# An attention kernel's steps in a new order: written out for all sixteen heads in place of one repeated turn

## The chip, the cores and the metric

One core of one Trainium2 chip. The time is that of the whole program on the device, in microseconds (us), the median of the runs; less is better. The five engines of the core each run a list of instructions in its order: TensorE (PE, with its weight loads as PEld), VectorE (DVE), ScalarE (ACT), GpSimd (POOL) and SyncE (SP), which here only starts transfers. They wait for one another by semaphores.

## What is computed

Two sequences of 512 tokens of width 256 pass through a feed-forward part, an attention and a second feed-forward part, each behind a layer norm and added to its input:

```python
x = x + 0.5 * ffn(layernorm(x))        # 16 experts, 4 per token, and a shared one
x = x + attention(layernorm(x))
x = x + 0.5 * ffn(layernorm(x))

# attention, for each of 16 heads of width 128
q, k, v = (silu(conv4(x @ W.T)) for W in (Wq, Wk, Wv))
s = statistics of (k @ Wsv.T) against v   # three numbers per token
beta, amp = sigmoid(mlp_b(s)), mlp_a(s)
g = -exp(A) * softplus(k / norm(k) * amp + dt_bias)
S = S * exp(g_t)[:, None]; S = S + k_t * ((v_t - k_t @ S) * beta_t); o_t = (q_t * scale) @ S
out = (rmsnorm(o) * norm_w * sigmoid(gate)) @ Wo.T
```

All of it is in float32. The recurrence over 512 tokens is computed in four chunks of 128 tokens per sequence.

## The kernel before

`program` gives each engine a function. Each goes through the first feed-forward part (`ffn_te`, `ffn_se`, ...), then the attention (`attention_sy`, `attention_te`, `attention_se`, `attention_ve`, `attention_ge`), then the second feed-forward part.

Inside an attention function every step of the computation is a small function of a head `h`, and often of a sequence `b` (0 or 1), a chunk `n` (0 to 3) or a level `l` (0 to 6). A step begins with its waits, `wait_ge(*signal.of(h, ...))`, issues a few instructions and lets the last count a signal up. `@live` leaves out a step whose head is not 0 to 15. The steps that the text speaks of:

- `p_k`, `p_v`, `p_q` (L1241): projections of a head, 8 matmuls of 512 columns. For nearly all heads they go to one pair of PSUM banks, FF. ACT takes the result out (`tap_k`, `tap_v`, `tap_q`, L2109 to L2123), scaled by the first weight of the convolution, and DVE adds the other three out of the same banks (`taps_k`, `taps_v`, `taps_q`, L2829, three instructions). Then `p_vT`, `p_kk`, `p_qq` (L1287, transposes) and `p_vhat` (L1281) use the same banks, with `v_rows`, `vhat_sq`, `k_sq`, `q_sq` on ACT and `err` on DVE emptying them.
- `t_lvl`, `t_diag`, `t_kT`: the matrices inside a chunk, by seven levels, in the banks L. Between levels DVE scales (`t_mkq`, L2985) and POOL multiplies (`t_dec`, L3549, L3551). `m_out`, `m_in` on SP, `substitute` on POOL and `t_out_w`, `t_out_t`, `t_in_m`, `t_in_t` on SP invert 16 x 16 blocks by way of HBM; `i_tx`, `i_ty` (L1438, L1441), `i_tr`, `i_last` on PE put the inverse together.
- `c_gate` (L1469), then for chunks 0 to 3 `c_p` (L1478), `c_u` (L1487) and `c_ko` (L1499 to L1502): the recurrence over the chunks, in the banks S, with `c_us`, `c_os` on ACT and `c_r`, `c_s` on DVE between them. It ends with `o_sq` (ACT), `o_sum` (DVE, L3054 to L3059), `o_pow`, `o_scale`, `o_norm` (POOL), `c_oT` (PE) and `c_fin` (DVE), which writes the head's output. `spill(h)` on SP saves it to HBM.
- `soft_abs`, `soft_exp`, `soft_log`, `soft_relu`, `soft_low`, `soft_res` (POOL, L3531 and L3534), `soft_sum`: the decay g. `silu_set` and `exp_set` load ACT's table for the functions that follow.
- The output projection, at the end of PE's list: `o_zero(q)` clears one of four banks, `o_part(h, lo, hi)` (L1515) adds the part of head `h` for four of the eight blocks of 128 tokens, 8 matmuls of 256 columns. 30 such half steps, for heads 0 to 14, stand in the list, and four `o_last(q)` add head 15. The outputs of heads 0 to 14 come back from HBM by `o_load_a` (heads 0 to 4), `o_load_b` (5 to 8), `o_load_c` (9 to 12) and `o_load_d` (13 and 14) on SP, each of which waits for a buffer to fall free in head 15: `o_load_b` for `i_done(15)`, `o_load_c` for `decay(15)`, `o_load_d` for the last level of head 15.

The order of the steps on each engine is written by hand in three functions: `begin()`, `turn(t)`, and `finish()`:

```python
begin()
for t in range(FIRST, LAST):      # 4 to 13
    turn(t)
finish()
```

`turn(t)` has one head's worth of steps on every engine, of several heads at once: on PE `p_q(t - 1)`, `t_lvl(t - 3, ...)`, `c_u(t - 4, ...)`. The loop is unrolled when the program is built. `finish()` has the steps of the last heads in an order of their own, on PE from the middle of `c_u` of head 10 on. In `turn`, the part of PE's list from `p_q` on is: last chunk of the recurrence with `g_norm`, `t_lvl(.., 1, 6)`, `p_vT`, `t_lvl(.., 0, 6)`, `p_vhat`, `i_tx`, `t_kT`, `i_ty(.., 4)`, `p_kk`, `i_tr`, `g_norm`, `c_oT`, `p_qq`, `i_tx(.., 5)`, `t_lvl(.., 0)`, `t_diag`, and the next turn's `p_k`, `i_ty(.., 5)`. At the end of `finish` PE has `o_part(0..4, 0, 4)` among the steps of head 14's recurrence, and after the last `c_ko` of head 15 the other 25.

Of the kernel before, what the change touches and what calls it, by code (L numbers as in the profile page):

```python
# [80 lines left out]
def program(nc, a, out):  # L81
    with ExitStack() as ctx:
# [922 lines left out]
        def attention_sy(sy):  # L1005
# [100 lines left out]
            def begin():  # L1106
                pass

            def turn(t):
                weights(t - 5)  # L1110
                gate_weights(t - 8)
                spill(t - 11)
                t_out_w(t - 9)
                t_out_t(t - 9)
                t_in_m(t - 9)
                t_in_t(t - 9)
                m_out(t - 8)
# [2639 lines left out]
```

How the kernel before makes its waits and increments, by code:

```python
        def sync(sy):  # L347
# [1 line left out]
                sy.dma_start(x[:, 2 * q:2 * q + 2, :], a["x"][2 * q * P:2 * (q + 1) * P].rearrange("(n p) d -> p n d", p=P))\  # L349
                    .then_inc(s_x[q], 16)
            shared_loads(sy)
            rows_out(sy, 0)
            expert_loads(sy, 0, E)
            for dst, src in ((wsv[:, :], a["WsvT"]), (lmask[:, :, :], a["lmask"]), (rmask[:, :, :], a["rmask"]),
                             (fmask[:, :], a["fmask"]), (dmask[:, :], a["dmask"]),
                             (pall[:, :, 0:NPAR - 1], a["par"]), (eye16[:, :], a["eye16"]),
                             (norm_w[:, :], a["norm_w"].rearrange("(m o) -> m o", o=1)), (wg1[:, :, :], a["Wg1T"])):
                sy.dma_start(dst, src).then_inc(s_const, 16)
            sy.wait_ge(zeroed, 1)
            for c in range(BN):
                for m, (w, bias) in enumerate((("Wb1", "bb1"), ("Wa1", "ba1"))):
                    at = (2 * (c % 2) + m) * MLP
# [8 lines left out]
                        .then_inc(s_const, 16)  # L371
            sy.dma_start(alog[:, :], a["A_log"].rearrange("(o m) -> o m", o=1).to_broadcast([P, NH])).then_inc(s_const, 16)
            for h in range(2):
                sy.dma_start(wqkv[:, h, :, :, :], a["wqkv"][h]).then_inc(s_w[h], 16)
            rows_in(sy, 0)
            sy.wait_ge(att_zero, 3)
            sy.dma_start(t_img.rearrange("s q x -> (s q x)").rearrange("(p x) -> p x", p=P), inv[:, 0:BN * IMAGE * 16 // P])\
                .then_inc(s_scr, 16)
```

## Time and profile before

| what | value |
|---|---|
| median of 3 runs | 1612.05 us (1611.71 to 1615.12) |
| span of the profiled execution, first to last instruction | 1569.7 us |
| instructions in the profile | 28651 |
| PE, DVE, ACT, POOL busy | 1360.0, 1060.1, 807.1, 687.8 us |
| chain that ended last | PE 67%, DVE 15%, ACT 6%, issue 5%, DMA 3%, POOL 2% |
| moved by the DMA engines | 117.04 MB |

Of the profiled execution only the span is given. The busy time of an engine is a sum over stages with different limits; which engine waits for which is to be read stage by stage. Times in the rows are from the start of the span.

### The profile page before, as it was taken

The page shows a single profiled execution, that of the slowest core. Times are in us where ns is not written, and L with a number is a line of the kernel's source. Part 1 is how long each engine was busy: PE and PEld are TensorE (multiplying, and loading weights), DVE is VectorE, ACT ScalarE, POOL GpSimd, SP SyncE. Part 2 cuts the span into 40 slices and gives each one's busy share as a digit, 9 for nine tenths or more (in the row PEclk, how much of TensorE's full clock was granted, in tenths as well). Part 3 has the DMA queues.
Part 4 walks back from the last instruction along what each step waited for, and adds up shares of the span by engine and source line. Part 5 has one row for each costly group of instructions (what it writes and reads, how often), then busy time and mean ns, then how long its engine had stood idle before and what let it go on. Part 6 is the DMA issues. An engine that isn't in the chain of part 4 may idle for free.

```text
span 1569.7 us, 28651 instructions
## 1 busy us (share of the span) xinstructions
PE 1360.0 (87%) x9424; PEld 1050.0 (67%) x9424; DVE 1060.1 (68%) x1981; ACT 807.1 (51%) x2597; POOL 687.8 (44%) x991
## 2 busy tenths in 40 slices
PE   7999757778989889898898898898977889899993
PEld 5777524557767767777676676687766667757772
DVE  5744366778868778889788888897774621265445
ACT  1122127576776766867767668678574332011220
POOL 0277700355354452554644535535455430005772
PEclk9899967899999999999999999999988989989997
DMA  9233320011120220211211311111013213242334
GB/s 359 61 104 103 115 99 20 16 43 34 36 61 17 56 71 15 58 30 46 67 32 31 84 30 32 45 48 51 17 46 110 88 46 148 103 209 71 105 102 174
DMA packets 130960, 117.04 MB, mean 75 GB/s; under 512 B 58944, under 2 KB 115328, under 8 KB 130048
## 3 DMA queue, kind: packets, MB, share of 16 engines
q1 hardware_dynamic: 121216, 90.20, 18.2%
q0 software_dynamic: 9024, 24.65, 5.4%
q8 instruction: 80, 1.31, 0.4%
q14 instruction: 64, 0.52, 0.1%
q10 hardware_dynamic: 576, 0.34, 0.1%
HBM read 80.30 MB, written 34.87 MB: 73 GB/s over the span
## 4 chain that ended last, share of the span: by engine, by line
PE 67%; DVE 15%; ACT 6%; issue 5%; DMA 3%; POOL 2%; DVEq 0%; SPq 0%; POOLq 0%; ACTq 0%
PE proj L1241 9%; DVE big L2829 6%; PE chain L556 5%; PE low L1383 5%; PE tree L1383 5%; PE gates L534 4%; PE low L534 3%; PE proj L1281 2%; PE proj L1287 2%; PE chain L1469 2%; PE tree L1427 2%; PE proj L1515 2%; PE tree L1452 2%; PE proj L471 2%; DVE x L903 2%
## 5 line engine op out<-in xcount | busy, mean ns | idle before, releaser
L3549 POOL TENSOR_TENSOR big<-big 128x512 f32<-128x512 f32 (+6 forms) x112 | 60.4, 539 | 378.2 <-PE tree L1392 123.5
L2829 DVE SCALAR_TENSOR_TENSOR big<-proj,pall,big 128x1022 f32<-128x1022 f32 x129 | 164.4, 1274 | 13.9 <-ACT big L2109 7.8
L1241 PE MATMUL proj<-xT,wqkv 128*128 128x512 f32 x344 | 158.8, 605 | 16.3 <-DVE big L2829 15.6
L2985 DVE TENSOR_TENSOR KQ<-KQ,big 128x1024 f32<-128x1024 f32 x112 | 150.3, 1342 | 17.3 <-PE low L1355 8.3
L980 POOL DMA_INDIRECT inv<-xn_scr,gidx x94 | 91.3, 971 | 135.2 <-DVE sidx L841 107.1
L3551 POOL TENSOR_TENSOR big<-big 128x512 f32<-128x512 f32 x112 | 145.4, 1298 | 0.0
L1241 PEld LDWEIGHTS proj<-xT,wqkv 128*128 128x128 f32 x344 | 63.2, 194 | 82.8 <-issue 63.1
L986 POOL DMA_INDIRECT y_scr<-inv,sidx x94 | 92.8, 987 | 37.0 <-issue 22.5
L626 ACT COPY big<-proj 128x256 f32<-128x256 f32 x94 | 35.2, 374 | 125.9 <-PE proj L523 125.8
L3563 POOL TENSOR_TENSOR prodw<-D,W 64x15 f32<-64x15 f32 (+7 forms) x240 | 89.4, 373 | 18.8
L1383 PE MATMUL low<-KQ,big 128*128 128x128 f32 x640 | 91.1, 286 | 7.6 <-POOL big L3551 4.0
L556 PE MATMUL chain<-big 88*128 x376 | 96.6, 380 | 0.0
L1383 PE MATMUL tree<-KQ,big 128*128 128x128 f32 x640 | 90.9, 286 | 1.2 <-POOL big L3551 0.9
L1383 PEld LDWEIGHTS low<-KQ,big 128*128 128x128 f32 x640 | 80.5, 195 | 12.7 <-issue 8.2
L3576 POOL TENSOR_TENSOR ot<-ot,of 128x1024 f32<-128x1024 f32 x16 | 30.4, 1898 | 131.9 <-DVE of L3065 131.9
L1383 PEld LDWEIGHTS tree<-KQ,big 128*128 128x128 f32 x640 | 82.8, 199 | 4.3 <-issue 2.9
L3566 POOL TENSOR_TENSOR W<-W,prodw 64x15 f32<-64x15 f32 (+7 forms) x240 | 76.1, 317 | 18.8
L1287 PE MATMUL proj<-ident,big 128*128 128x128 f32 x384 | 57.8, 300 | 30.2 <-DVE big L2829 12.6
L1287 PEld LDWEIGHTS proj<-ident,big 128*128 128x128 f32 x384 | 47.2, 154 | 38.2 <-issue 22.4
L556 PEld LDWEIGHTS chain<-big 88*128 88x128 f32 x376 | 63.9, 190 | 5.5
L534 PE MATMUL gates<-big 128*128 x192 | 65.0, 461 | 0.6 <-issue 0.6
L3531 POOL TENSOR_TENSOR big<-big 128x1024 f32<-128x1024 f32 x16 | 37.7, 2359 | 60.9 <-DVE big L2949 60.9
(311 smaller groups left out, 3649.2 us busy)
## 6 DMA issues: line engine op xcount, KB each, us to landing
big<-in_w_ex SPq DMA_DIRECT2D x2, 4864.0 KB, 20.8
big<-in_w_ex SPq DMA_DIRECT2D x2, 4256.0 KB, 18.7
big<-y_scr SPq DMA_DIRECT2D x8, 1024.0 KB, 8.2
m_img<-big SPq DMA_DIRECT2D x16, 512.0 KB, 3.2
inv<-t_img SPq DMA_DIRECT2D x16, 512.0 KB, 4.2
big<-t_img SPq DMA_DIRECT2D x16, 512.0 KB, 5.1
o_scr<-obuf SPq DMA_DIRECT2D x15, 512.0 KB, 4.0
wqkv<-in_wqkv SPq DMA_DIRECT2D x16, 384.0 KB, 3.8
```

Source lines behind the costliest of these rows:

```text
L534: t = te.matmul(bank[2 + j % 2][:, 0:2 * INTER], xgT[:, j % 2, k, :], big[:, bass.ds(at + k * 2 * INTER, 2 * INTER)], start=(k == 0), stop ...
L556: t = te.matmul(bank[6 + j % 2][:, 0:H], aT[0:INNER, j % 2, i, :], big[0:INNER, bass.ds(at + KB * 2 * INTER + i * H, H)], start=(i == 0), ...
L980: ge.indirect_dma_start(out=xg[:, j % GOT, :], out_offset=None, in_=xn_scr[f], in_offset=bass.IndirectOffsetOnAxis(ap=gidx[:, j:j + 1], ax ...
L986: ge.indirect_dma_start(out=y_scr[f], out_offset=bass.IndirectOffsetOnAxis(ap=sidx[:, j:j + 1], axis=0), in_=ob[:, j % PUT, :], in_offset= ...
L1241: m = te.matmul(place(h, j)[:, b, :], wqkv[:, h % 2, j, k, :], xT[:, k, b * T:(b + 1) * T], start=(k == 0), stop=(k == KB - 1))
L1287: m = te.transpose(FF[:, c // NC, c % NC * P:(c % NC + 1) * P], v[:, c * P:(c + 1) * P], ident[:, :])
L1383: m = te.matmul(dst, suf[:, c * P:(c + 1) * P], right, start=True, stop=True)
L2829: ve.scalar_tensor_tensor(conv[:, :, d:T], place(h, j)[:, :, 0:T - d], pall[:, h, 4 * j + 3 - d:4 * j + 4 - d], conv[:, :, d:T], ALU.mult, ...
L2985: ve.tensor_tensor(kr, kr, dl, ALU.mult).then_inc(mkq.sem, 1)
L3551: ge.tensor_tensor(left, left, d[:, :, 1].unsqueeze(2).to_broadcast([P, M, 1 << l]), ALU.mult)\
L3563: ge.tensor_tensor(prodw[:, 0:rows, 0:k], D[:, j, j + 1:SUB].unsqueeze(2).to_broadcast([BN * 8, rows, k]), W[:, j, 0:k].unsqueeze(1).to_br ...
L3566: ge.tensor_tensor(W[:, j + 1:SUB, 0:k], W[:, j + 1:SUB, 0:k], prodw[:, 0:rows, 0:k], ALU.subtract)\
```

## The change

`begin`, `turn` and `finish` are gone from all five attention functions, and the steps stand in one list for all sixteen heads. The step functions and their waits are the same, and each step is there as often as before; only its place differs. `silu_set` and `exp_set` lose their argument, and there is one call more of each (36 and 36, where there were 35 and 35), in the first heads. A head's steps now stand in a slightly different order from head to head. On POOL only places of `soft_res`, `t_dec(.., 6)` and `o_norm` change. The feed-forward parts are as before.

On PE, among others: `i_ty(h - 2, 5)` stands ahead of `p_k(h + 1)` instead of behind it for h = 4 to 9 and 12, and a `c_gate(h - 2, ...)` for h = 5, 11 and 12. `p_v` of heads 10, 12 and 13 stands further back, near to `p_q`. On ACT `q_sq` is ahead of `v_sq` in 7 heads; on DVE the two `c_fin` of a head mostly stand together. From `c_u(14, 1, 0)` on, the whole of PE's list is below, and of the SP list the end. A line of "..." stands for what is left out of the 5138 lines.

```diff
@@ -1103,125 +1103,155 @@
-            def begin():
-                pass
-
-            def turn(t):
-                weights(t - 5)
-                gate_weights(t - 8)
-                spill(t - 11)
-                t_out_w(t - 9)
-                t_out_t(t - 9)
-                t_in_m(t - 9)
-                t_in_t(t - 9)
-                m_out(t - 8)
-                m_in(t - 8)
-
-            def finish():
-                spill(3)
-                t_out_w(5)
-                t_in_m(5)
-                t_out_t(5)
-                t_in_t(5)
-                gate_weights(6)
-                weights(9)
-                m_out(6)
-                m_in(6)
-                spill(4)
-                t_out_w(6)
-                t_out_t(6)
...
-                o_load_a()
-                m_out(15)
-                m_in(15)
-                t_out_w(15)
-                spill(13)
-                t_out_t(15)
-                t_in_m(15)
-                t_in_t(15)
-                gate_weights(15)
-                o_load_b()
-                spill(14)
-                o_load_c()
-                o_load_d()
-                spill(15)
-
...
+            o_load_a()
+            m_out(15)
+            o_load_c()
+            m_in(15)
+            t_out_w(15)
+            t_in_m(15)
+            spill(13)
+            t_out_t(15)
+            t_in_t(15)
+            spill(14)
+            o_load_d()
...
@@ -1543,551 +1573,1180 @@
-            def turn(t):
-                g_amp(t - 2, 0)
-                c_u(t - 4, 1, 1)
-                c_p(t - 4, 0, 1)
...
-                c_u(15, 1, 3)
-                c_u(15, 0, 3)
-                c_ko(15, 1, 3)
-                c_ko(15, 0, 3)
-                o_part(5, 0, 4)
-                o_part(6, 0, 4)
-                o_part(7, 0, 4)
-                o_part(8, 0, 4)
-                o_part(9, 0, 4)
-                o_part(10, 0, 4)
-                o_part(11, 0, 4)
-                o_part(12, 0, 4)
-                o_part(13, 0, 4)
-                o_part(14, 0, 4)
-                c_oT(15, 0)
-                o_zero(2)
-                o_zero(3)
-                o_part(0, 4, 8)
-                o_part(1, 4, 8)
-                o_part(2, 4, 8)
-                o_part(3, 4, 8)
-                o_part(4, 4, 8)
-                o_part(5, 4, 8)
-                o_part(6, 4, 8)
-                o_part(7, 4, 8)
-                o_part(8, 4, 8)
-                o_part(9, 4, 8)
-                c_oT(15, 1)
-                o_part(10, 4, 8)
-                o_part(11, 4, 8)
-                o_part(12, 4, 8)
-                o_part(13, 4, 8)
-                o_part(14, 4, 8)
-                o_last(0)
-                o_last(1)
-                o_last(2)
-                o_last(3)
...
+            p_k(10)
+            i_tr(7, 0, 5)
+            t_lvl(8, 1, 1)
...
+            c_u(7, 0, 0)
+            c_ko(7, 1, 0)
+            c_ko(7, 0, 0)
+            t_lvl(8, 1, 4)
+            c_p(7, 1, 1)
+            g_amp(9, 1)
+            t_lvl(8, 0, 4)
+            c_u(7, 1, 1)
+            c_p(7, 0, 1)
+            p_v(10)
+            c_u(7, 0, 1)
+            c_ko(7, 1, 1)
+            t_lvl(8, 0, 5)
+            c_ko(7, 0, 1)
+            c_p(7, 1, 2)
+            c_p(7, 0, 2)
+            t_lvl(8, 1, 5)
+            c_u(7, 0, 2)
+            c_u(7, 1, 2)
+            c_ko(7, 1, 2)
+            c_ko(7, 0, 2)
+            p_q(10)
+            c_p(7, 0, 3)
...
+            c_u(14, 1, 0)
+            t_lvl(15, 0, 4)
+            c_u(14, 0, 0)
+            t_lvl(15, 1, 4)
+            c_ko(14, 0, 0)
+            c_p(14, 0, 1)
+            c_ko(14, 1, 0)
+            o_zero(2)
+            c_u(14, 0, 1)
+            o_zero(1)
+            o_part(2, 0, 4)
+            c_p(14, 1, 1)
+            t_lvl(15, 1, 5)
+            c_ko(14, 0, 1)
+            o_part(3, 0, 4)
+            c_u(14, 1, 1)
+            o_part(11, 0, 4)
+            c_ko(14, 1, 1)
+            t_lvl(15, 0, 5)
+            o_part(0, 0, 4)
+            c_p(14, 0, 2)
+            c_p(14, 1, 2)
+            c_u(14, 0, 2)
+            c_u(14, 1, 2)
+            c_ko(14, 1, 2)
+            c_ko(14, 0, 2)
+            o_part(1, 0, 4)
+            c_p(14, 0, 3)
+            o_part(4, 0, 4)
+            c_p(14, 1, 3)
+            t_lvl(15, 0, 6)
+            t_lvl(15, 1, 6)
+            c_u(14, 0, 3)
+            c_u(14, 1, 3)
+            c_ko(14, 1, 3)
+            c_ko(14, 0, 3)
+            i_tx(15, 1, 4)
+            i_tx(15, 0, 4)
+            o_part(9, 0, 4)
+            i_ty(15, 4)
+            o_part(10, 0, 4)
+            i_tr(15, 0, 4)
+            c_oT(14, 0)
+            t_kT(15, 1)
+            i_tr(15, 1, 4)
+            c_oT(14, 1)
+            t_kT(15, 0)
+            i_tx(15, 0, 5)
+            i_tx(15, 1, 5)
+            c_gate(15, 1)
+            i_ty(15, 5)
+            o_zero(3)
+            o_part(1, 4, 8)
+            i_tr(15, 0, 5)
+            c_gate(15, 0)
+            i_tr(15, 1, 5)
+            o_part(12, 4, 8)
+            i_tx(15, 1, 6)
+            i_tx(15, 0, 6)
+            o_part(0, 4, 8)
+            i_last(15)
+            o_part(3, 4, 8)
+            c_u(15, 0, 0)
+            c_u(15, 1, 0)
+            o_part(13, 4, 8)
+            c_ko(15, 1, 0)
+            c_ko(15, 0, 0)
+            o_part(4, 4, 8)
+            c_p(15, 1, 1)
+            c_p(15, 0, 1)
+            o_part(7, 0, 4)
+            c_u(15, 0, 1)
+            c_u(15, 1, 1)
+            o_part(5, 4, 8)
+            c_ko(15, 1, 1)
+            c_ko(15, 0, 1)
+            o_part(5, 0, 4)
+            c_p(15, 0, 2)
+            o_part(11, 4, 8)
+            c_p(15, 1, 2)
+            c_u(15, 0, 2)
+            o_part(8, 0, 4)
+            c_u(15, 1, 2)
+            c_ko(15, 0, 2)
+            c_ko(15, 1, 2)
+            o_part(9, 4, 8)
+            c_p(15, 0, 3)
+            c_p(15, 1, 3)
+            o_part(13, 0, 4)
+            c_u(15, 0, 3)
+            c_u(15, 1, 3)
+            o_part(2, 4, 8)
+            c_ko(15, 0, 3)
+            c_ko(15, 1, 3)
+            o_part(12, 0, 4)
+            o_part(14, 0, 4)
+            o_part(8, 4, 8)
+            o_part(6, 0, 4)
+            c_oT(15, 0)
+            c_oT(15, 1)
+            o_part(7, 4, 8)
+            o_part(10, 4, 8)
+            o_part(14, 4, 8)
+            o_part(6, 4, 8)
+            o_last(0)
+            o_last(1)
+            o_last(2)
+            o_last(3)
...
```

## Rows read from the trace of the kernel before

**Rows 1.** The page, part 1: busy us (share of the span) xinstructions.

```profile
PE 1360.0 (87%) x9424; PEld 1050.0 (67%) x9424; DVE 1060.1 (68%) x1981; ACT 807.1 (51%) x2597; POOL 687.8 (44%) x991
```

**Rows 2.** Windows by stage: us, busy us (instructions) per engine, PEclk, DMA share, GB/s.

```profile
223.50:350.00 126.50, 93.85 (x518) 64.11 (x519) 86.09 (x115) 82.90 (x303) 34.90 (x50) 0.87 0.09 25
350.00:1098.90 748.90, 675.77 (x5658) 537.49 (x5657) 622.43 (x956) 531.80 (x1777) 364.35 (x588) 0.98 0.17 44
1098.90:1249.90 151.00, 125.76 (x1034) 104.11 (x1033) 101.78 (x165) 81.00 (x233) 70.31 (x106) 0.90 0.22 67
1249.90:1313.50 63.60, 51.88 (x400) 41.89 (x400) 16.49 (x40) 22.10 (x62) 15.62 (x39) 0.89 0.36 120
1313.50:1362.20 48.70, 48.70 (x228) 42.15 (x228) 4.64 (x12) 3.11 (x5) 1.90 (x1) 1.00 0.14 51
```

**Rows 3.** Windows of one head: p_q(10), p_kk(10), (p_k(11)), p_v(11) to p_q(11), the sum.

```profile
824.32:842.40 18.08, 15.02 (x108) 11.90 (x109) 15.30 (x19) 14.94 (x45) 11.91 (x18) 1.00 0.27 66
842.40:853.21 10.81, 9.41 (x103) 8.22 (x102) 9.53 (x14) 10.22 (x62) 1.90 (x1) 1.00 0.01 3
...
871.00:886.20 15.20, 13.60 (x111) 10.10 (x109) 11.76 (x25) 8.18 (x18) 9.14 (x25) 1.00 0.34 105
sum 61.88, PE 55.81 PEld 44.21 DVE 52.87 ACT 44.25 POOL 30.01; mean PE 13.95 PEld 11.05 DVE 13.22 ACT 11.06 POOL 7.50
```

**Rows 4.** Waits of PE from 605 to 1038: us in total, times, longest.

```profile
PE proj L1287 <- DVE big L2829: 6.9, 7, 1.2
PE proj L1241 <- DVE big L2829: 6.6, 7, 1.1
```

**Rows 5.** Timeline, head 10's tap_v, taps_v and p_q: start us, us, what.

```profile
815.66 1.12 ACT L2115 ACTIVATE big<-proj,pall 128x1024 f32<-128x1024 f32 x1
820.36 3.90 DVE L2829 SCALAR_TENSOR_TENSOR big<-proj,pall,big 128x1022 f32<-128x1022 f32 x3
824.32 3.70 PE L1241 MATMUL proj<-xT,wqkv 128*128 128x512 f32 x8 [1.12 <-DVE big L2829]
```

**Rows 6.** Windows from p_v to p_q: head 14, then head 10.

```profile
1055.23:1063.98 8.75, 7.87 (x47) 5.58 (x45) 7.38 (x13) 5.33 (x11) 3.66 (x9) 1.00 0.44 127
809.08:824.32 15.24, 13.64 (x111) 10.15 (x109) 11.79 (x25) 8.17 (x18) 9.19 (x25) 1.00 0.26 78
```

**Rows 7.** Groups by line, ACT: table loads, count, busy us, mean ns, idle.

```profile
L2337 ACT ACT_TABLE_LOAD x35 | 44.9, 1283 | 0.6
```

**Rows 8.** Timeline, PE after head 15's recurrence: six half steps, 48 matmuls.

```profile
1320.45 10.52 PE L1515 MATMUL proj<-big 128*128 128x256 f32 x48
```

**Rows 9.** Windows inside the stage of 63.6 us.

```profile
1249.90:1285.00 35.10, 28.54 (x244) 24.06 (x243) 9.05 (x22) 12.10 (x38) 15.62 (x39) 1.00 0.21 53
1285.00:1300.30 15.30, 12.98 (x88) 9.27 (x89) 3.40 (x5) 5.08 (x9) 0.00 (x0) 0.55 0.18 61
```

**Rows 10.** Groups by line, PE, 1285 to 1300.3: count, busy us, mean ns, idle.

```profile
L1469 PE MATMUL chain<-g,wg 128*128 128x512 f32 x4 | 3.6, 1064 | 0.0
```

**Rows 11.** The same group from 853 to 1038.

```profile
L1469 PE MATMUL chain<-g,wg 128*128 128x512 f32 x12 | 6.4, 619 | 0.0
```

**Rows 12.** Timeline, SP: m_out(15), m_in(15), o_load_b: start us, us of issuing, what.

```profile
1247.15 0.37 SPq L1024 DMA_DIRECT2D m_img<-big  x1
1250.35 0.60 SPq L1031 DMA_DIRECT2D D<-m_img  x1
...
1296.52 1.76 SPq L1082 DMA_DIRECT2D inv<-o_scr  x4
```

**Rows 13.** Timeline, PE behind p_k(10): one i_ty(7, 5).

```profile
794.86 0.69 PE L1441 MATMUL tree<-inv,big 32*32 32x32 f32 x32
```

**Rows 14.** Windows from p_k(13) to p_k(14) and from there to p_k(15).

```profile
976.50:1038.50 62.00, 56.28 (x512) 45.17 (x511) 52.88 (x83) 43.34 (x144) 32.22 (x50) 1.00 0.17 46
1038.50:1098.90 60.40, 54.14 (x423) 43.15 (x422) 49.88 (x77) 46.18 (x152) 28.34 (x49) 0.97 0.17 47
```

**Rows 15.** Line L3056, o_sum's product of 8 elements: ns min/median/max.

```profile
L3056 DVE TENSOR_TENSOR of<-rq x16: 152/701/1926, 392.2 to 1316.3; 128x8 f32<-128x8 f32 x16
```

**Rows 16.** Line L3534, soft_res's second step: ns min/median/max.

```profile
L3534 POOL TENSOR_TENSOR big<-big x16: 2344/2356/2392, 275.7 to 1215.7; 128x1024 f32<-128x1024 f32 x16
```

More of the change, by code:

```diff
@@ L2087, in attention_te @@
-            begin()
-            for t in range(FIRST, LAST):
-                turn(t)
-            finish()
+            p_k(0)
+            p_v(0)
+            p_q(0)
+            p_k(1)
+            p_vT(0)
+            p_vhat(0)
+            p_v(1)
+            p_kk(0)
+            p_qq(0)
+            p_q(1)
+            g_sT(0)
+            g_hid(0)
+            g_z(0)
+            g_amp(0, 0)
+            p_vT(1)
+            g_amp(0, 1)
+            p_vhat(1)
+            c_gate(0, 1)
+            g_norm(0, 0)
@@ new lines, in attention_te @@
+            c_u(1, 0, 3)
+            c_u(1, 1, 3)
+            c_ko(1, 1, 3)
+            g_norm(3, 0)
+            c_ko(1, 0, 3)
+            t_lvl(2, 0, 6)
+            p_vT(4)
+            t_lvl(2, 1, 6)
+            p_vhat(4)
+            i_tx(2, 0, 4)
+            i_tx(2, 1, 4)
+            t_kT(2, 1)
+            t_kT(2, 0)
+            i_ty(2, 4)
+            p_kk(4)
+            g_norm(3, 1)
+            i_tr(2, 0, 4)
+            c_oT(1, 0)
+            c_oT(1, 1)
+            p_qq(4)
@@ new lines, in attention_te @@
+            p_q(6)
+            c_p(3, 0, 3)
+            c_p(3, 1, 3)
+            c_u(3, 1, 3)
+            c_u(3, 0, 3)
+            c_ko(3, 1, 3)
+            g_norm(5, 0)
+            c_ko(3, 0, 3)
+            p_vT(6)
+            t_lvl(4, 1, 6)
+            t_lvl(4, 0, 6)
+            p_vhat(6)
+            i_tx(4, 1, 4)
+            i_tx(4, 0, 4)
+            t_kT(4, 0)
+            i_ty(4, 4)
+            p_kk(6)
+            i_tr(4, 0, 4)
+            t_kT(4, 1)
+            g_norm(5, 1)
@@ L2812, in attention_se @@
-            begin()
-            for t in range(FIRST, LAST):
-                turn(t)
-            finish()
+            tap_k(0)
+            tap_v(0)
+            silu_set()
+            silu_k(0)
+            tap_q(0)
+            silu_v(0)
+            tap_k(1)
+            v_rows(0)
+            silu_q(0)
+            vhat_sq(0)
+            v_sq(0)
+            tap_v(1)
+            k_sq(0)
+            e_sq(0)
+            q_sq(0)
+            exp_set()
+            powers(0)
+            tap_q(1)
@@ L3521, in attention_ve @@
[L3521 to L3524 removed]
+            taps_k(0)
+            taps_v(0)
+            taps_q(0)
+            taps_k(1)
+            err(0)
+            red_abs(0)
+            taps_v(1)
+            red_all(0)
+            roots(0)
+            cosines(0)
+            taps_q(1)
+            mlp_out(0)
+            amps(0)
+            g_raw(0, 0)
+            g_raw(0, 1)
+            soft_low(0)
+            soft_relu(0)
```

4750 lines of the change are left out of this document (3192 added, 1558 removed).

## The prediction

> **What bounds the kernel now.** I read the page's busy shares first. TensorE (PE) is busy 87% of the 1569.7 us span, VectorE (DVE) 68%, ScalarE (ACT) 51%, GpSimd (POOL) 44% [rows 1]. A share over the whole span hides stages with different limits, so next come the windows by stage [rows 2]. The two feed-forward parts (before 223.5 and after 1362.2) are not touched by the change. The attention lies between, 1138.7 us, in five stages: the filling (126.5 us, PE idle 32.7), the steady heads (748.9 us, idle 73.1), the running out (151.0 us, idle 25.2, clock 0.90), the recurrences of heads 14 and 15 (63.6 us, idle 11.7) and a final stretch of 48.7 us in which PE is never idle.
>
> One steady head, from one p_q to the next, takes 61.9 us, of which PE works 55.8 [rows 3]. No order of the same work takes that away, so a better order can gain 6 us a head at most. The four stretches of one head say where the idle time is: 3.1 us between p_q and p_kk, 1.4 between p_kk and the next p_k, none between p_k and p_v, 1.6 between p_v and p_q [rows 3]. The waits name the cause: in seven heads PE waited about 1 us before p_q and about 1 us before p_vT, each time for DVE's conv taps, L2829 [rows 4]. All seven PE steps of a head's q, k and v go through one pair of banks, so they form a chain: p_v, tap_v 1.1, taps_v 3.9, p_q 3.7 and on. Yet taps_v began 3.6 us after tap_v had ended, because other work stood ahead of it on DVE [rows 5]. From p_v to p_q this takes 15.24 us in a head of the repeated turn, and 8.75 in head 14, whose order is already written out on its own [rows 6].
>
> **The change, part by part.** It removes no arithmetic and no transfer. It adds two table loads on ACT: 72 switches of the set instead of 70, at 1.28 us each [rows 7], 2.6 us in heads 1 to 3 on an engine that works 82.9 of 126.5 us there [rows 2]. The engine's 43.6 us idle cover them, so I count 0; without that cover they would cost 2.6.
>
> **The end of the attention** is the one place where the order differs in kind. The output projection is 30 half steps o_part(h, lo, hi) plus o_last. Six of them took 10.52 us back to back [rows 8], so one is 1.75 us. Before, 5 stand among the steps of head 14's recurrence and 25 behind c_ko(15, 0, 3). After, 12 stand between the first c_u of head 14 and the first of head 15, 10 among the steps of head 15's recurrence, and 8 behind its last c_ko. So 17 half steps, 29.8 us, leave the final stretch: 7 (12.3 us) go into the 50.4 us up to 1300.3, where PE is idle 6.6 + 2.3 = 8.9 us [rows 9], and 10 (17.5 us) into the 13.2 us that remain of the stage, with the rest of its 11.7 us idle, 2.8 [rows 2]. What doesn't fit lengthens those stretches by at least 3.4 and 14.7 us. The most this part can give by filling is 29.8 - 3.4 - 14.7 = 11.7 us, just the idle time. The gaps are 0.2 to 3 us and a half step is 1.75, so it can't all be had; I take 60%, 7 us. The result still needs its last c_fin: after the last c_ko come square, sum, powers, scale, o_norm and two transposes, and 8 half steps (14 us) cover them, so nothing new waits there.
>
> In the same place the granted clock was low, 0.55 from 1285 to 1300.3, so nearly all of it at the lower level of 1.2 GHz, right after a stretch in which PE worked 28.5 of 35.1 us [rows 9]. At that clock one c_gate matmul took 1064 ns [rows 10], against 619 at full clock [rows 11]. If the filled order keeps the clock up, 13.0 us of work becomes 13.0 x 619/1064 = 7.6, a gain of 5.4; if not, 0. I take 3, for half of it. Together **-10 us**, ends -17 and 0. The Trainium skill (TensorE: Matmul & The Clock Gate, What's actually happening) says that low clock is the default and activity lifts it; by that rule the fuller order keeps it and this part is -12 instead of -10. No run here shows it yet.
>
> What hides the loads for these half steps: SP issues o_load_c (four transfers) between m_out(15) and m_in(15). Before, m_in(15) went out 3.2 us after m_out(15), waiting for it to land [rows 12]. The issues fit that wait; the bytes may hold m_in(15) a few us, which head 14's steps on PE cover. o_load_d is now ahead of o_load_b, and o_load_b no longer ahead of spill(14); before, both waited till 1296.5 [rows 12].
>
> **The steady heads, 3 to 13.** Of the PE list I compared what stands between p_q(h) and p_k(h + 1), where 4.5 of a head's idle 6 us lie. i_ty(h - 2, 5), 0.7 us [rows 13], is moved into it in 7 of the heads 3 to 12, and a c_gate (two matmuls of 619 ns, about 1.0 overlapped) in 3: 4.9 + 3.0, about 8 us in all. In the turn i_ty stands right behind p_k and is ready hardly earlier, so it can't fill the gaps ahead of it, and I count half: -4 us. On the other engines q_sq goes ahead of v_sq in 7 heads and both c_fin stand together; no PE step waits for these now: 0. In heads 10, 12 and 13 p_v stands later, with 9.2, 8.1 and 7.6 us of PE work up to p_q (the steps listed between them, each at its median in the trace) instead of 13.6; head 14 shows that this can hold [rows 6]. Heads whose order is already their own bound the stage: 62.0 and 60.4 us [rows 14] against 61.9. So one head may gain 1.5 us, or, by one more wait of the size met before p_q and p_vT [rows 4], lose 1: over 11 heads -17 to +11. I take **-4**, nearer to the first of the two.
>
> **Filling and running out.** The order of heads 0 to 2 is nearly the same: 0, ends -4 and +3. From 1098.9 to 1249.9 PE is idle 25.2 us at clock 0.90, but no output half step can come there, since the loads wait for head 15's diagonal steps; only the order of heads 12 to 14 differs. I take **-2**, ends -8 and +4.
>
> **Sum.** -10 - 4 + 0 - 2 = -16 us. The profiled span is 1569.7 us; the median of the runs shown is 1612.05, so 42.35 us lie around the span, and they stay. 1569.7 - 16 = 1553.7 of span, 1596.0 us in all.
>
> **The rivals.** *Forecast*, chance 0.50: the filled end shows, the heads gain a little, 1582 to 1606.
>
> *More of it*, 0.14: the filling works fully, the clock stays up and the heads are as good as the one of 60.4 us. -17 - 16 - 4 = -37: 1575 us. For it: head 14 [rows 6, 14]. Against: the other head with its own order took 62.0.
>
> *The end is blocked*, 0.14: o_part(13, 4, 8) stands ahead of c_ko(15, 1, 0), and it needs c_fin(14), spill(14) landed, then o_load_d. If that arrives 6 us late the whole recurrence stands still, and o_part(7, 0, 4) behind o_load_b may do the same. 10 - 6 = 4 is left, and with the heads at 0 the time is 1612 - 4 - 2 = 1606 us. For it: four transfers on one queue. Against: c_oT(14) now stands about 16 us of PE work ahead of that half step.
>
> *The late p_v*, 0.13, ends slower: if in heads 10, 12 and 13 ACT and DVE take up taps_v as late as in the repeated turn, the 15.24 us between p_v and p_q [rows 6] stay while PE has 9.2, 8.1 and 7.6 us of work, and it stalls 6.0, 7.1 and 7.6 us. +21 on the forecast: 1617 us. It decides from a mean stall of 5.3 us a head on, where the 16 us are eaten. Against it is head 14, which was idle 0.9 us there.
>
> *Engines in each other's way*, 0.09. o_sum's product of 8 elements takes 152 ns at best but 701 in the median and 1926 at worst [rows 15]; o_sum runs while soft_res, two steps of 2356 ns, runs on POOL [rows 16]. A new order can put such a DVE step ahead of the taps. One hit is worth up to 2.4 us less the 1.4 that DVE is idle before its err step, 1.0 a head, +11 in all: 1607 us. The Trainium skill (SBUF — State Buffer, Summary: rules for kernel authors) has it that a DVE operation with two SBUF inputs and a GpSimd one that reads SBUF exclude each other, the later one standing still; the 1926 ns agree.
>
> **How the numbers follow.** About 0.2%, 3.2 us, is what a measurement of this kernel can tell from no change. Faster: the forecast 0.50, more of it 0.14, half of the blocked end 0.07, a third of the collisions 0.03: 0.74. Same: 0.07 + 0.03 + 0.02 = 0.12. Slower: 0.11 of the late p_v and 0.03 of the collisions: 0.14. The range goes from 1574, just under the larger gain, to 1616, under the late p_v; what lies outside is about 0.06 on each side. The likeliest case's own range is 1582 to 1606.
>
> **What would show it.** Right: 8 half steps of L1515 behind the last c_ko of head 15 and 22 before; the final stretch near 49 - 30 = 19 us; PE idle between the first c_u of head 14 and the last c_ko below 5 us, where it was 11.7; a clock above 0.9 in it; steady heads of 61 to 62 us. Wrong: PE idle over 2 us before o_part(13, 4, 8); p_v to p_q over 11 us in heads 10, 12 or 13; steady heads above 62.5 or below 60.5; new half-clock stretches between 350 and 1098.9.

## The result, and the profile after

The change made the kernel slower: 1656.61 us in the median of 4 runs (1652.38 to 1665.98) against 1613.59 us for the kernel before (1611.71 to 1616.98), a ratio of 1.0267 with a 95% interval of 1.0232 to 1.0302. The forecast was 1596.0, its range ended at 1616.

The page of the kernel after, its lines that answer to [rows 1]:

```profile
span 1664.2 us, 28653 instructions
...
PE 1399.9 (84%) x9424; PEld 1092.2 (66%) x9424; DVE 1107.8 (67%) x1981; ACT 806.2 (48%) x2599; POOL 685.5 (41%) x991
...
L5240 POOL TENSOR_TENSOR big<-big 128x512 f32<-128x512 f32 (+6 forms) x112 | 64.6, 577 | 468.6 <-PE tree L1413 135.6
L4161 DVE TENSOR_TENSOR KQ<-KQ,big 128x1024 f32<-128x1024 f32 x112 | 167.0, 1491 | 15.4 <-PE tree L1385 4.9
```

The same instructions in another order take longer: DVE is busy 1107.8 us instead of 1060.1, PE 1399.9 instead of 1360.0. All of DVE's 47.7 us are the order's, since a run in before's order (`flat`, below) has DVE at 1059.9. That run has PE at 1383.3, so only some 17 of PE's 40 us are the order's, and the rest is a matter of the execution that was profiled. L4161 is `t_mkq` (L2985 before), where one instruction went from 1342 to 1491 ns in the mean.

By stage, the rows of the kernel after that answer to [rows 2]: the ten heads from p_k(4) to p_k(14), then the recurrences of heads 14 and 15 up to the last c_ko, then the final stretch. The columns are us, busy time of each engine with its instructions, granted clock, DMA share and GB/s.

```profile
452.90:1112.00 659.10, 579.05 (x4768) 467.41 (x4767) 540.43 (x801) 441.20 (x1467) 303.98 (x490) 0.95 0.16 43
1337.60:1417.90 80.30, 75.00 (x548) 64.49 (x548) 17.65 (x41) 22.20 (x63) 14.69 (x39) 1.00 0.30 100
1417.90:1436.00 18.10, 18.10 (x88) 15.65 (x87) 5.34 (x13) 3.12 (x5) 2.39 (x2) 1.00 0.37 135
```

And of `flat`, the first experiment, which has before's order and shows it in an execution like the others:

```profile
432.70:1065.00 632.30, 570.96 (x4769) 455.78 (x4768) 522.92 (x803) 441.15 (x1478) 303.90 (x491) 0.98 0.17 44
1277.60:1341.30 63.70, 51.96 (x401) 42.03 (x400) 16.50 (x40) 22.06 (x62) 15.56 (x39) 0.89 0.36 120
1341.30:1390.50 49.20, 49.20 (x229) 42.24 (x227) 5.33 (x13) 3.12 (x5) 2.38 (x2) 1.00 0.13 50
```

The end does what was forecast: 112.9 us became 98.4. The ten heads do not: 659.1 against 632.3. Heads 1 to 3 lose as well: from p_k(1) to p_k(4) it is 176.4 us in `flat` (256.3 to 432.7) and 196.7 after (256.2 to 452.9).

### The profile page after: what moved, and what is told of

Same layout as the page of the kernel before. It is cut to its first block and busy times, and to the rows that moved or that the text cites. A ratio compares the mean times of both kernels' runs of the same rounds, so it can differ in the third digit from the quotient of the medians.

```text
span 1664.2 us, 28653 instructions
## 1 busy us (share of the span) xinstructions
PE 1399.9 (84%) x9424; PEld 1092.2 (66%) x9424; DVE 1107.8 (67%) x1981; ACT 806.2 (48%) x2599; POOL 685.5 (41%) x991
## 5 line engine op out<-in xcount | busy, mean ns | idle before, releaser
L4161 DVE TENSOR_TENSOR KQ<-KQ,big 128x1024 f32<-128x1024 f32 x112 | 167.0, 1491 | 15.4 <-PE tree L1385 4.9
L1271 PE MATMUL proj<-xT,wqkv 128*128 128x512 f32 x344 | 161.3, 613 | 11.9 <-DVE big L4005 11.2
L5242 POOL TENSOR_TENSOR big<-big 128x512 f32<-128x512 f32 x112 | 140.4, 1253 | 0.0
L1271 PEld LDWEIGHTS proj<-xT,wqkv 128*128 128x128 f32 x344 | 64.8, 199 | 79.4 <-issue 64.8
L1413 PE MATMUL low<-KQ,big 128*128 128x128 f32 x640 | 97.2, 299 | 19.9 <-DVE KQ L4161 9.3
L1413 PE MATMUL tree<-KQ,big 128*128 128x128 f32 x640 | 98.7, 302 | 12.8 <-DVE KQ L4141 4.2
L1413 PEld LDWEIGHTS low<-KQ,big 128*128 128x128 f32 x640 | 86.4, 207 | 28.9 <-issue 13.0
L1413 PEld LDWEIGHTS tree<-KQ,big 128*128 128x128 f32 x640 | 89.6, 213 | 23.7 <-issue 10.9
L1317 PE MATMUL proj<-ident,big 128*128 128x128 f32 x384 | 62.5, 316 | 29.5 <-DVE big L4005 18.2
L5257 POOL TENSOR_TENSOR W<-W,prodw 64x15 f32<-64x15 f32 (+7 forms) x240 | 78.9, 329 | 18.8
L5254 POOL TENSOR_TENSOR prodw<-D,W 64x15 f32<-64x15 f32 (+7 forms) x240 | 69.8, 291 | 18.8
L1317 PEld LDWEIGHTS proj<-ident,big 128*128 128x128 f32 x384 | 52.2, 164 | 35.8 <-DVE big L4005 20.4
L2969 ACT COPY U<-chain 128x128 f32<-128x128 f32 x128 | 32.1, 266 | 83.4 <-PE chain L1517 82.4
```

Source lines behind the costliest of these rows:

```text
L1271: m = te.matmul(place(h, j)[:, b, :], wqkv[:, h % 2, j, k, :], xT[:, k, b * T:(b + 1) * T], start=(k == 0), stop=(k == KB - 1))
L1317: m = te.transpose(FF[:, c // NC, c % NC * P:(c % NC + 1) * P], v[:, c * P:(c + 1) * P], ident[:, :])
L1413: m = te.matmul(dst, suf[:, c * P:(c + 1) * P], right, start=True, stop=True)
L4161: ve.tensor_tensor(kr, kr, dl, ALU.mult).then_inc(mkq.sem, 1)
L5242: ge.tensor_tensor(left, left, d[:, :, 1].unsqueeze(2).to_broadcast([P, M, 1 << l]), ALU.mult)\
L5254: ge.tensor_tensor(prodw[:, 0:rows, 0:k], D[:, j, j + 1:SUB].unsqueeze(2).to_broadcast([BN * 8, rows, k]), W[:, j, 0:k].unsqueeze(1).to_br ...
```

## The experiments

All steps of the attention can be cut in time by where they began in the trace of before, and each section can have either kernel's order: the steps ahead of a cut need nothing from behind it. In what follows "steady" is the section from 350 to 1098.9 us of before's trace. The step functions are the same text everywhere; in `flat`, `mid_a`, `end_a` and their variants their lines are those of the kernel after, less 2 from L3010 on.

**Which part of the order costs.** `flat` is before's order written out. `head_a`, `mid_a` and `end_a` have after's order in one section each:

```diff
-begin(); turn(4) ... turn(13); finish()
+flat:    every step of before, in before's order, in one list
+head_a:  steps that begin before 350 us in after's order, the rest in before's
+mid_a:   steps that begin from 350 to 1098.9 us in after's order
+end_a:   steps that begin from 1249.9 us on in after's order
```

> The order of before on every engine, but written out like after. Theory 'the order costs': the same instructions in the same places, so within 3 us of before, about 1613 us. Rival 'it is not the order' (something in how the longer list reaches the engines, or the two runs compared were of different conditions): 1630 to 1656 us. The profile also tells whether the feed-forward parts, 20 us longer each in after's profile (attention begins at 243.4 instead of 223.5, and 237.7 us lie behind its last step instead of 217.6), are longer with before's order too: then those 40 us are a matter of the execution that was profiled and no effect of the change.

Measured 1612.56 us against 1610.97 (ratio 1.0008, 0.9986 to 1.0031): writing the order out costs nothing. The attention began at 243.5 us of its profile as in after's.

> After's order for the steps that begin before 350 us (heads 0 to 2), before's order for the rest. Theory 'filling': p_k to p_k took 5, 11 and 6 us longer for heads 1, 2 and 3 in after, so if the first heads' own order is the cause, about 15 to 20 us slower than before (1630). Theory 'steady heads': 0 to +3 us, since the longer periods of heads 1 to 3 would come from elsewhere.

Measured 1625.80 us, ratio 1.0104 (1.0071 to 1.0138): about +15 (+13 against `flat`). The first heads do cost something.

> After's order for the steps that begin between 350 and 1098.9 us (the steady heads), before's order ahead of and behind them. Theory 'steady heads': most of the 43 us, +30 to +45 (1643 to 1658). Theory 'filling': these heads alone cost +15 to +25, the rest stands in the first heads. My forecast had -4 for this part.

Measured 1654.49 us, ratio 1.0285 (1.0255 to 1.0314): +43.5 against before, +41.9 against `flat`. As much as the whole loss.

> Before's order up to 1249.9 us, after's from there on: the output half steps in the recurrences of heads 14 and 15, nothing else. My forecast's term: -10 us (1603). Rival 'the end is blocked': -4 or worse. By after's profile, from p_k(15) to its last c_fin 249.1 us against 253.2, -4 us.

Measured 1595.89 us, ratio 0.9924 (0.9900 to 0.9948): -15. This kernel beats both. In sum 15 + 43.5 - 15 = 43, which is what the change cost.

**Where the steady heads lose.** `end_a` has before's order in all of the attention up to the recurrences of heads 14 and 15, so its profile can be laid beside that of `mid_a`. First `mid_a`, then `end_a`: from the first p_k to p_k(15), and the ten heads alone.

```profile
243.20:1160.80 917.60, 786.16 (x6175) 623.73 (x6176) 736.76 (x1070) 615.13 (x2079) 400.06 (x638) 0.94 0.15 40
439.60:1095.30 655.70, 576.81 (x4768) 465.67 (x4767) 540.29 (x801) 440.51 (x1467) 303.69 (x490) 0.96 0.16 43
```

```profile
243.30:1118.20 874.90, 770.40 (x6174) 602.83 (x6175) 708.99 (x1070) 614.81 (x2078) 399.25 (x638) 0.97 0.16 41
430.30:1057.70 627.40, 566.89 (x4768) 450.59 (x4767) 520.69 (x802) 441.47 (x1478) 305.85 (x491) 0.98 0.17 45
```

The long stretch is 42.7 us longer in `mid_a`, about the whole loss. 26.9 us of it are idle time of PE (131.4 against 104.5). In the other 15.8 us PE works longer on the same matmuls, at a mean granted clock of 0.94 instead of 0.97.

PE's waits from p_k(4) to p_k(14), the longest rows in `flat` (us in total, times, longest; L1271 is a projection, L1317 a transpose behind it, L1385 and L1413 are `t_lvl`, L1517 `c_u` and L1529 `c_ko`):

```profile
PE proj L1317 <- DVE big L4003: 10.5, 10, 1.2
PE proj L1271 <- DVE big L4003: 10.0, 10, 1.1
PE tree L1385 <- issue: 5.8, 9, 1.3
PE low L1385 <- ACT big L2930: 5.7, 4, 1.8
```

and in `mid_a`:

```profile
PE proj L1317 <- DVE big L4003: 12.8, 9, 1.9
PE chain L1529 <- ACT U L2969: 8.3, 10, 1.6
PE chain L1517 <- DVE R L4209: 7.8, 17, 0.8
PE proj L1271 <- DVE big L4003: 5.3, 6, 1.6
PE low L1413 <- DVE KQ L4159: 4.4, 6, 1.1
...
PE low L1385 <- DVE KQ L4159: 2.7, 2, 2.0
PE tree L1413 <- DVE KQ L4159: 2.4, 4, 0.7
```

The waits before the projections (L1271) halved, from 10.0 to 5.3 us. In its place come waits for `t_mkq` (L4159) and for the recurrence's `c_r` and `c_us`. The row of `t_mkq` alone tells it apart: duration in ns (lowest, median, highest), and then who waited for it. In `flat` nobody did:

```profile
L4159 DVE TENSOR_TENSOR KQ<-KQ,big x71: 1210/1218/2446, 431.5 to 1063.6; 128x1024 f32<-128x1024 f32 x71
```

in `mid_a` PE did, for 12.7 us (the four rows of PE added):

```profile
L4159 DVE TENSOR_TENSOR KQ<-KQ,big x70: 1208/1224/3195, 439.6 to 1080.2; 128x1024 f32<-128x1024 f32 x70
...
  PE low L1413: 4.4, 6
  PE tree L1413: 4.0, 5
...
  PE low L1385: 2.7, 2
...
  PE tree L1385: 1.6, 1
```

An instruction that normally takes 1.22 us took up to 3.2. Two stretches of `mid_a`'s timeline, DVE and POOL, show what it stands for (start us, duration us):

```profile
943.00 2.35 POOL L5220 TENSOR_TENSOR big<-big 128x1024 f32<-128x1024 f32 x1
945.50 2.36 POOL L5223 TENSOR_TENSOR big<-big 128x1024 f32<-128x1024 f32 x1
```

```profile
943.20 2.18 DVE L4230 TENSOR_TENSOR of<-rq 128x8 f32<-128x8 f32 x1
945.49 0.17 DVE L4233 TENSOR_TENSOR of<-of 128x8 f32<-128x8 f32 x1
945.62 2.27 DVE L4190 COPY cd<-big 128x8 f32<-128x8 f32 x1
947.80 0.67 DVE L4112 TENSOR_TENSOR big<-big,gates 128x512 f32<-128x512 f32 x1
```

`o_sum`'s and `chunk_decay`'s 8-column instructions (0.16 us when alone) both begin inside a product of `soft_res` on POOL and end with it. Here is one that PE paid for:

```profile
548.12 2.35 POOL L5220 TENSOR_TENSOR big<-big 128x1024 f32<-128x1024 f32 x1
548.54 2.02 DVE L4206 TENSOR_SCALAR R<-big,sqb 128x128 f32<-128x128 f32 x1
...
550.48 1.21 DVE L4159 TENSOR_TENSOR KQ<-KQ,big 128x1024 f32<-128x1024 f32 x1
...
551.75 1.12 PE L1385 MATMUL low<-KQ,big 128*64 128x128 f32 x8 [1.98 <-DVE KQ L4159]
```

`c_r` of a first chunk (L4206, 0.28 us when alone) stands still 1.7 us, `t_mkq` behind it comes late, and PE is idle 1.98 us.

I counted a DVE instruction as stretched when it took over 150 ns more than the lower quartile of its kind (same line and shape), over p_k(4) to p_k(14). `flat` has 43 of them, 26.1 us too long in all, 14.5 us of it in `o_sum`, for which no PE step waits soon. `mid_a` has 57, 46.4 us, and they lie elsewhere: `t_mkq` 16.7, `chunk_decay` 8.6, `roots` 5.5, `c_r` 4.1, `o_sum` only 2.9. The count hangs a little on how the quartile is taken: taken within the ten heads it is 36 instructions and 24.0 us for `flat`, 58 and 47.0 for `mid_a`. Each overlapped a POOL instruction, and about nine tenths of the time fell beside `t_dec` and `soft_res`. `t_mkq` was stretched in `flat` too (23 times, 9.4 us), but nobody waited for it there.

**Taking the collisions away.** First `soft_res` was cut to 8 columns (`res8`), then `t_dec`'s second product as well (`both8`), in before's order (`flat_`) and with the steady heads in after's (`mid_`):

```diff
-ge.tensor_tensor(t1, yv, t1, ALU.subtract)
+ge.tensor_tensor(t1[:, 0:8], yv[:, 0:8], t1[:, 0:8], ALU.subtract)
...
-ge.tensor_tensor(left, left, d[:, :, 1]..., ALU.mult)
+ge.tensor_tensor(left[:, 0:4, 0:1], left[:, 0:4, 0:1], d[:, 0:4, 1]..., ALU.mult)
```

`soft_res`'s second product is cut like its first. All kernels with `res8`, `both8`, `set` or `tiny` in their names leave out part of the decay g and of its products in this way.

> Before's order, with soft_res on POOL cut from 1024 to 8 columns (the decay g is then not the reference's), so that two steps of 2356 ns shrink to about 0.1 us. In before's order soft_res meets mostly o_sum on DVE, for which nobody waits. Both theories: within 3 us of before, 1608 to 1613.

> The steady heads in after's order, soft_res cut to 8 columns in the same way. It is to be read against the run of before's order with the same cut; mid_a with the full soft_res was 43 us above before. Theory 'collisions' (a DVE step that starts while a POOL product runs stands still till it ends, and in after's order such steps feed PE: in heads 4 to 13 they are 46 us longer in all against 26 us, of which 19.8 meet soft_res): the difference falls to about 28 us. Theory 'the order of PE itself' (waits that arise from where the steps stand): it stays at 38 to 43.

> Before's order, with soft_res cut to 8 columns and the second product of t_dec (L3551, 1.3 us) cut to 4 columns; what is computed is then not the reference. Hardly any long POOL product is left in a head but the first two of t_dec and o_norm. Theory 'collisions': a little faster than before, 1595 to 1610, since its own 26 us of stretched DVE steps go too, most of them on o_sum, where they cost nothing.

> The steady heads in after's order with both cuts, to be read against before's order with both cuts. Theory 'collisions': the difference of 43 us falls to 15 or less. Theory 'the order of PE itself': 35 or more stays. Between them: both share the loss, and the part that goes is the price of the collisions.

| steady heads in after's order, and base | stretched DVE time, heads 4 to 13 | medians | difference |
|---|---|---|---|
| full products | 46.4 us (base 26.1) | 1654.49, 1612.56 | +41.9 |
| `soft_res` cut | 26.2 (8.5) | 1635.03, 1610.77 | +24.3 |
| both cut | 4.0 (3.0) | 1603.44, 1609.31 | -5.9 |

The base of the first row is `flat`; against before itself it is +43.5. With these cuts the base did not move from before by more than its interval (1.0008, 0.9992 to 1.0025, and 0.9987, 0.9966 to 1.0007). The two bases further below were a little faster, 0.9975 (0.9961 to 0.9989) with memsets and 0.9971 (0.9946 to 0.9997) with small pieces. So the collisions of before's order cost between nothing and some 4 us. The loss of the steady heads went with the collisions, and what stayed is a gain (`mid_both8`: 0.9956, 0.9935 to 0.9976). The waits of PE for `t_mkq` fell from 12.7 us in `mid_a` to 3.0 in `mid_both8`. The expectation "15 or less" was too careful.

**DVE standing still, or POOL late?** The cuts also made POOL's results come earlier. Memsets of the same tiles were to keep POOL's time:

```diff
-ge.tensor_tensor(left, left, d[:, :, 1]..., ALU.mult)
+ge.memset(left, 1.0)
```

> Before's order, where soft_res on POOL and the second product of t_dec are replaced by a memset of the same tile (values then not the reference's): POOL is busy about as long but reads no operand from SBUF. Expected of every theory: within 1% of before. It is the base for the next run; its profile shows how long such a memset takes and whether DVE steps beside it are stretched.

> The steady heads in after's order with the same memsets, against before's order with them. With both products cut to a few columns this difference had fallen from +43 to -6 us. Theory 'collisions' (DVE stands still beside a POOL product): no more than 10 us, if the memset doesn't hold DVE up and its stretched steps stay below 10 us. Rival 'POOL is late' (the cut helped because POOL's results came 1 us earlier each, not because DVE was free): the difference comes back to 30 or more wherever the memsets are as long as the products were.

Measured 1608.10 and 1595.76 us, a difference of -12. But a memset of 512 columns took 0.54 us where the product takes 1.2 to 1.3, so POOL was early again, and the rival's condition wasn't met. What it does show stands in the last section. Small pieces keep POOL's time better: 12 products of 8 columns for each of `soft_res`'s, 6 of one column for `t_dec`'s second.

```diff
+for k in range(12):
+    w = slice(8 * k, 8 * k + 8)
+    r = ge.tensor_tensor(t1[:, w], yv[:, w], t1[:, w], ALU.subtract)
```

> Before's order. Each of soft_res's two products is replaced by 12 products of 8 columns, t_dec's second product by 6 of one column (what is computed is not the reference's). A small product took about 200 ns on POOL, so POOL is busy about as long as with the full ones, but in pieces. Base for the next run: within 1% of before.

> The steady heads in after's order with the same small pieces; this tells whether DVE's standing still or POOL's own time made the loss. Theory 'collisions': a DVE step waits for one piece at most, its stretched steps stay under 10 us in all, and the difference to before's order with the same pieces is between -12 and 0 us. Rival 'POOL is late': POOL is as long as with the full products, so the difference is 30 us or more.

In `mid_tiny` `soft_res` took 5.7 us from first to last instruction (5.9 in `mid_a`) and `t_dec` 1.83 (1.77), so POOL was as late as ever, while the stretched DVE time was 3.9 us. Measured 1616.83 us in the median of nine runs (a tenth, of 7324 us, is left out; ratio to before 1.0004, 0.9974 to 1.0034) against 1611.24 (0.9971, 0.9946 to 0.9997): +5.6 us, within about 6. That is above the -12 to 0 that was expected, and far from the rival's 30. So 36 of the 41.9 us against `flat`, or 38 of the 43.5 against before, go when DVE no longer stands still, with POOL as late as ever. The 11 us between this +5.6 and the -5.9 of the cut products may be POOL's time, if they are more than the measurement's width.

**The first heads, and the whole.** `head_both8` is `head_a`, `after_both8` the kernel after, each with both cuts of above and no other edit.

> After's order for heads 0 to 2 only, both POOL products cut, against before's order with both cut (1609). With full products this part cost 15 us. Theory 'collisions everywhere': 0 to +3 us. The sum of parts in the whole of after with both cuts (1590.5 = 1609.3 - 6 - 15 + rest) says +2. Rival 'the filling has its own waits' (heads 1 to 3 begin with PE idle a third of the time): +10 to +15.

Measured 1619.46 us, ratio to before 1.0019 (0.9993 to 1.0045), to be read against `flat_both8`'s 0.9987: +5 us where it was +15, between what the two theories gave. In the profiles, the stretch from the first p_k to p_k(4) is 189.2 us in `flat`, 199.3 in `head_a` and 189.2 in `head_both8`, with PE idle 38.9, 45.0 and 39.7; DVE's stretched time there is 1.2, 7.4 and 0.2. About 10 of the 15 us are the same cause. 5 stay open, hardly more than can be measured; the two table loads more on ACT, 2.6 us, lie in these heads, and no run took them out.

> The whole of after with both POOL products cut. If collisions are nearly all of the loss and the parts add up: 1609 (before's order with both cuts) - 6 (steady heads) - 15 (end) and 0 to +15 for the first heads, so 1588 to 1603 us, where after is 1656. Rival 'the first heads cost something else': 1603. If the cut did its work only in the steady heads by chance, above 1610.

Measured 1590.50 us, ratio 0.9852 (0.9830 to 0.9873). The whole of after, without the two long POOL products, is 19 us faster than before's order without them (1609.31; 22 us by the ratios, since the two were measured apart, each beside before), where with them it is 43 slower.

**The running out.**

> Before's order up to 1098.9 us, after's for all that begins later, the running out and the end together; nothing cut. The end alone (from 1249.9 us) gave 15 us. My forecast had -2 for the running out: 1594. By collisions it can also lose: heads 13 and 14 in after's order have new stretched steps like those of the steady heads (2 to 4 us a head), which would give 1598 to 1602.

Measured 1597.37 us (0.9905, 0.9876 to 0.9935), against 1595.89 for the end alone: the running out adds nothing that can be measured.

**POOL's own changed order.** `m_three` is `mid_a` with before's order kept on POOL and SP, so it tests both engines' order at once.

> The steady heads with after's order on PE, ACT and DVE but before's on POOL and SP, nothing cut: on POOL soft_res stands ahead of t_dec(.., 6) again for heads 6, 8, 9 and 11, where after has it behind. There chunk_decay (DVE, 159 ns) ran into soft_res and took about 2 us each time. Theory 'the swap on POOL is the main cause': most of the 43 us goes, 1625 or less. Theory 'collisions all over' (57 stretched steps, four of them these): 3 to 8 us less than the 1654.5 of the steady heads with after's POOL order, since the rest stays; or none, since t_dec(.., 6) then comes up to 4.7 us later behind soft_res.

Measured 1668.09 us (1.0331, 1.0313 to 1.0349). It was measured beside a before of 1614.93, so it is 53 us above before where `mid_a` is 43.5 (by the ratios 7 us more than `mid_a`), and neither value fits. In its ten heads PE is idle 91.6 us, in `mid_a`'s 78.9. The swap on POOL is no cause of the loss: beside the other engines' new order, moving `soft_res` behind `t_dec(.., 6)` makes `chunk_decay` collide and seems to pay all the same. The likely reason is the one named last, that `t_dec(.., 6)` otherwise comes a `soft_res` (4.7 us) later; no run took it by itself, nor POOL's order without SP's.

**Shorter holds, with all of it computed.** The whole of after, with long products split:

```diff
+for k in range(4):
+    w = slice(256 * k, 256 * (k + 1))
+    r = ge.tensor_tensor(t1[:, w], yv[:, w], t1[:, w], ALU.subtract)
...
+for k in range(2):
+    w = slice(M // 2 * k, M // 2 * (k + 1))
+    r = ge.tensor_tensor(left[:, w], left[:, w], d[:, w, 1]..., ALU.mult)
```

> The whole of after, computing all of it, with soft_res's two products in 4 pieces of 256 columns each and t_dec's second product in 2 halves. Theory 'collisions': a DVE step can slip in between two pieces, so the longest stretch falls from 2.3 us to about 0.7 and the 46 us of heads 4 to 13 to about 25; after's 1656 us would fall to 1625 to 1640. If DVE's stretched steps matter only by their sum and the pieces add their own overhead, or if DVE waits for the whole train of pieces: 1650 or more.

Measured 1662.38 us, ratio 1.0299 (1.0220 to 1.0378): no gain on after's 1.0267, and not the 1625 to 1640 of the theory. The longest stretch fell from 2.2 to 1.3 us and the stretched DVE time to 32.6, so DVE does slip in between pieces. But there were 73 stretched instructions, and POOL paid: `soft_res` took 6.9 us from first to last instead of 5.9, `t_dec` 2.19 instead of 1.77. PE was idle 81.0 us in the ten heads (80.1 in after's). Splitting seems to trade holds for lateness, and here to be worth nothing; no run took the two apart.

## Why the prediction was wrong

**The end of the attention, -10 (ends -17 and 0): right.** Measured -15. From the first c_u(14) to the end of o_last, `flat` takes 112.9 us and the kernel after 98.4. Of the 14.5 us, 6.4 are idle time filled (11.7 to 5.3; I had 7), and 8.1 are PE work that went faster (51.96 + 49.20 to 75.00 + 18.10), since the half-clock stretch of [rows 9] is gone: clock 1.00 instead of 0.89. I had taken 3 of 5.4 us for that; it measured 8.1 here and 6.0 in `end_a`, so this term was too small and makes up most of what the part gave beyond -10. 8 half steps stand behind the last c_ko and the final stretch is 18.1 us, where 19 was forecast. The Trainium skill (TensorE: Matmul & The Clock Gate, What's actually happening) has the low clock as the default, which activity lifts. The trace agrees, with 0.89 becoming 1.00 here and 0.96 in `end_a`, and the -12 worked out by that rule is nearer to the -15.

**The steady heads, -4 (ends -17 and +11): wrong, and this is the step that failed.** Measured +43. The sum counted what moved on PE's list and put the other engines at nothing, with "no PE step waits for these now: 0". That looked at two moves, `q_sq` and `c_fin`, while 577 of the 960 steps in DVE's list of the attention stand at another place in `mid_a`, and it took for granted that an instruction takes as long in the new order as in the old. `t_mkq` shows what this missed: no PE wait stood against it before, and 12.7 us did afterwards. What I priced by order alone was also a question of which instructions of DVE and POOL run at the same time, and before's order had that solved: over half of its stretched time fell on `o_sum`, and most of the rest on `t_mkq` where nobody waited for it. With collisions away, the new order measured -6, close to the -4 of the sum. That is luck as far as the profiles tell: the sum had gaps of PE filled, but in the ten heads PE is idle 61.5 us in `mid_both8` and 61.2 in its base.

**The first heads, 0 (ends -4 and +3): wrong.** Measured +15. "Nearly the same order" was no reason: 43 steps of PE's list and 43 of DVE's stand at another place in `head_a`. Two thirds of it were the same cause.

**The running out, -2:** at most 3 us either way, not told from zero.

**"42.35 us lie around the span, and they stay": wrong.** Every profile taken since has a span 1.8 us below its own time (`flat`: 1619.9 and 1621.68). The 1569.7 us span of before's profile was an execution with shorter feed-forward parts, 431.0 us in all where `flat` has 472.9, and its own time is not among the runs shown. Its attention began at 223.5 us; in every other profile, before's order or after's, it began at 242 to 246. Since only differences inside the attention were used, the forecast didn't suffer by it.

**The rivals.** *Engines in each other's way* had the mechanism and the wrong price: one hit of 1.0 us a head, +11, chance 0.09. There were about six a head (57 in ten), they hit steps that feed PE, and the price was 36 to 38 us in the steady heads and some 10 in the first. The row that could have told was there: 701 ns in the median for a 152 ns instruction [rows 15] means that half of these instructions already stood still in before's order, at a place where it is free. *The late p_v* didn't happen: 11.3, 9.1 and 8.7 us from p_v to p_q in heads 10, 12 and 13, with PE idle for 2.2, 1.7 and 1.6 of them where the rival had 6.0, 7.1 and 7.6 (its sign, over 11 us, was just met in head 10, without the stall). *The end is blocked* didn't either. Two signs named for a wrong forecast came true: steady heads above 62.5 us (65.9 in the mean) and more time at the lower clock in them (0.95 over the ten heads). Neither says which step of the sum was wrong.

## What to carry to other kernels

This is one kernel, but the check is cheap. Before reordering a kernel in which VectorE and GpSimd both work from SBUF, list the VectorE instructions whose highest duration is far above their lowest, and what GpSimd ran beside each. Such a list says which collisions the present order hides; a new order must be priced for the pairs that it puts side by side, for the waits alone don't show them. And judge parts apart: the same change held -15 us at the end and +43 in the middle, and the part that gains can be kept by itself.

## What the runs showed of the hardware

**Which DVE instructions stand still.** In `mid_a`, heads 4 to 13, instructions that began while a long POOL product ran took, against the same line alone: `chunk_decay` (copy from and to SBUF, L4190) 1888 ns against 163, `c_r` of a first chunk (scaling by a column, L4206) 1042 against 275, `t_mkq` (two SBUF inputs) 1769 against 1236 in the mean. Those with an operand in PSUM were untouched: the taps (L4003) 1277 against 1275, 17 of 90 times beside a product, and `c_r` of the later chunks (L4209) 345 against 344. So were reductions (L4228, 1219 against 1209). With memsets on POOL (`mid_set`), `t_mkq` was free, 9 times 1208 to 1226 ns beside one, but `chunk_decay` still took up to 1001 ns:

```profile
L4190 DVE COPY cd<-big x10: 163/172/1001, 475.6 to 1031.9; 128x8 f32<-128x8 f32 x10
```

The Trainium skill (SBUF — State Buffer, Who interferes with whom) says just this: two SBUF inputs contend with GpSimd reads only, while a copy or a scaling by a scalar in its two-port mode contends with any GpSimd instruction. The rows above agree. For the scaling beside a memset there is one row only, 350 ns for `c_r` in `mid_set`, and no trace here shows in which mode an instruction ran.

**The clock within one order.** The same ten heads, in the same order, don't all run at full clock in each execution. Head 11, first in `flat`, then in `end_a`:

```profile
875.80:941.40 65.60, 58.71 (x475) 47.59 (x475) 53.00 (x81) 44.17 (x150) 30.01 (x49) 0.95 0.19 50
```

```profile
872.30:934.10 61.80, 55.68 (x475) 44.19 (x474) 53.16 (x82) 43.99 (x149) 30.06 (x49) 1.00 0.20 53
```

The stretch at the lower clock cost 3.8 us in this head, and one profile can't tell it from an effect of the order. Of the 23.4 us by which `mid_a`'s ten heads are longer than `flat`'s, 17.6 are PE idle (61.3 to 78.9) and 5.8 PE busy longer, at a clock of 0.96 against 0.98. Against `end_a`'s ten heads it is 28.3, of which 18.4 are idle.

Over several executions the lower clock does go with the holds. The mean granted clock of the whole program was 0.923 to 0.926 in the four executions of `mid_a`. It was 0.931 to 0.944 in the ten of `flat`, 0.929 to 0.938 in the ten of `flat_both8` and 0.937 to 0.941 in the five of `mid_both8`, which has `mid_a`'s order on every engine. So part of what the holds cost seems to come as slower matmuls and not as idle time; no run held the clock still to price that part.
